# Weighted sums of two blocks in a row, behind the single-pass products of both blocks

## What is computed

```python
sim = jnp.einsum('bhid,bhjd->bhij', q * SCALE, k)          # n = 1024
sim = jnp.where(causal_mask, jnp.finfo(sim.dtype).min, sim)
attn = jax.nn.softmax(sim, axis=-1)
out = jnp.einsum('bhij,bhjk->bhik', attn, values)
```

## Time and profile before

| | us |
|---|---|
| median of 3 runs | 1012.2 |
| lowest, highest | 1009.75, 1013.5 |
| the profiled execution | 1008.53 |
| its span, first to last instruction | 1006.7 |

### The profile page before, as it was taken

How to read it: one execution, slowest core, us unless ns; L and a number is a source line. 1 busy time by engine, 2 the same in 40 slices (tenths; PEclk the granted TensorE clock), 3 DMA queues, 4 the chain that set the end, 5 groups by cost and what they waited for, 6 DMA issues and landing times.

```text
span 1006.7 us, 14712 instructions
## 1 busy us (share of the span) xinstructions
PE 946.7 (94%) x5620; PEld 734.5 (73%) x5620; DVE 684.6 (68%) x1051; ACT 392.1 (39%) x683; POOL 239.2 (24%) x261
## 2 busy tenths in 40 slices
PE   5879989999999999989999899999999999999997
PEld 3448868888755565689996687788876666659997
DVE  2555757546656778788876675665575767879786
ACT  5424556312266557510104346540204755761000
POOL 6211324123433214145610013220012201311000
PEclk9988999999999999999999999999999999999999
DMA  6112100252135430235541000012221000023663
GB/s 226 29 42 74 53 1 2 70 175 83 55 126 207 145 130 23 73 109 168 174 143 68 1 1 1 2 49 84 84 84 42 23 21 1 22 74 88 195 191 103
DMA packets 33848, 81.56 MB, mean 81 GB/s; under 512 B 5956, under 2 KB 10660, under 8 KB 33780
## 3 DMA queue, kind: packets, MB, share of 16 engines
q1 hardware_dynamic: 32500, 76.44, 23.4%
q10 hardware_dynamic: 1280, 4.20, 1.6%
HBM read 61.26 MB, written 19.20 MB: 80 GB/s over the span
## 4 chain that ended last, share of the span: by engine, by line
PE 73%; DVE 11%; ACT 4%; issue 4%; DMA 3%; POOL 2%; SPq 2%; ACTq 0%; DVEq 0%; POOLq 0%
PE ps L1054 17%; PE ps L1352 10%; PE ps L1289 6%; PE ps L1357 5%; PE ps L1204 4%; PE ps L1249 4%; DVE region L948 3%; PE ps L1062 3%; PE ps L1265 3%; PE ps L1156 3%; PE ps L1218 3%; PE ps L1171 2%; PE ps L1325 2%; PE ps L1326 2%; SPq L303 2%
## 5 line engine op out<-in xcount | busy, mean ns | idle before, releaser
L1289 PE MATMUL ps<-region 128*128 128x512 f32 (+3 forms) x384 | 161.4, 504 | 0.0
L927 DVE TENSOR_REDUCE region<-ps 128x1 f32<-128x512 f32 (+1 forms) x192 | 98.1, 550 | 65.7 <-PE ps L1268 65.7
L715 ACT ACTIVATE region<-ps 128x512 f32<-128x512 f32 x192 | 92.3, 487 | 125.1 <-PE ps L1328 113.6
L972 DVE COPY_PREDICATED region<-region,ps 128x512 f32<-128x512 uint32 x112 | 82.0, 736 | 71.9 <-PE ps L1054 71.3
L1352 PE MATMUL ps<-expert_hi,kst 128*128 128x256 f32 x512 | 126.1, 284 | 3.5 <-DVE kst L1002 2.5
L1352 PE MATMUL ps<-expert_lo,kst 128*128 128x256 f32 x512 | 124.4, 281 | 0.0
L1054 PE MATMUL ps<-expert_hi,wide_hi 128*128 128x512 f32 x256 | 102.6, 401 | 0.0
L1352 PEld LDWEIGHTS ps<-expert_hi,kst 128*128 128x128 f32 x512 | 97.2, 190 | 4.5 <-DVE kst L1002 2.9
L1054 PE MATMUL ps<-expert_hi,wide_lo 128*128 128x512 f32 x256 | 100.0, 391 | 0.0
L1054 PE MATMUL ps<-expert_lo,wide_hi 128*128 128x512 f32 x256 | 99.8, 390 | 0.0
L519 ACT ACTIVATE region<-ps 64x512 f32<-64x512 f32 (+4 forms) x146 | 80.9, 557 | 47.1 <-PE ps L1171 20.0
(11 more groups left out here) (143 smaller groups left out, 1797.0 us busy)
## 6 DMA issues: line engine op xcount, KB each, us to landing
region<-hot_rows SPq DMA_DIRECT2D x128, 128.0 KB, 3.4
expert_hi<-halves_kept SPq DMA_DIRECT2D x24, 512.0 KB, 3.7
expert_lo<-halves_kept SPq DMA_DIRECT2D x24, 512.0 KB, 4.8
halves_kept<-expert_hi SPq DMA_DIRECT2D x16, 512.0 KB, 2.7
halves_kept<-expert_lo SPq DMA_DIRECT2D x16, 512.0 KB, 3.9
expert<-in_value_experts SPq DMA_DIRECT2D x8, 512.0 KB, 5.0
expert<-in_output_experts SPq DMA_DIRECT2D x8, 512.0 KB, 5.1
gb<-gate_rows ACTq DMA_DIRECT2D x16, 256.0 KB, 3.8
```

The source lines that it names most:

```text
L715: act.activation(PT[:, g % RING, lo:CH], ps[:, 4 + g % 2, 0:CH - lo], ACT.Exp).then_inc(sem["pt_ready"], 1)
L927: dve.tensor_reduce(mx[:, i, at_mx:at_mx + 1], ps[:, max_bank(h, m), 0:w], AX.X, ALU.max).then_inc(sem["s_max"], 1)
L972: dve.copy_predicated(V3_heads[:, t], chosen.unsqueeze(3).broadcast_to([P, PAIRS3, 2, HD3]), ps[:, n % 4, :].rearrange("p (a i k) -> p a i ...
L1289: mm(ps[:, SUM_BANK[c], lo:CH], V3[:, j, h // 2, h % 2 * HD3:(h % 2 + 2) * HD3], PT[:, g % RING, lo:CH], start=(j == 0), stop=(j == TC * ( ...
```

## The change

In PE's loop over the blocks the call of weigh moves. Before, each block's transposed scores were followed at once by the sum of the block two before, and then by the projection, the scores and the row of maxima that the tables put there. Now a block with even n is followed by its projection and scores alone; a block with odd n by its projection and scores, then by the sums of the blocks three and two before it, then by the row of maxima. Every instruction of every engine stays, and the order on the other engines too.

```diff
                         last.then_inc(sem["st_ps"], 1)
-                        if g >= LAG:
-                            weigh(g - LAG)
                         if n in PROJECT_AT and h % 2 == 0 and h + 2 < H3:
                             project(h // 2 + 1, PROJECT_AT.index(n))
                         if h + 1 < H3:
                             for m in SCORES_AT.get(n, ()):
                                 scores(h + 1, m)
-                            if n == MAX_ROW_AT:
-                                max_rows(h + 1)
+
+                        if n % 2:
+                            for k in (g - 1 - LAG, g - LAG):
+                                if k >= 0:
+                                    weigh(k)
+                        if h + 1 < H3 and n == MAX_ROW_AT:
+                            max_rows(h + 1)
 
                 for g in range(H3 * NB - LAG, H3 * NB):
                     weigh(g)
```

## The result

| | before | after |
|---|---|---|
| median, us | 1011.3 | 1020.93 |
| lowest, highest, us | 1009.75, 1013.5 (4 runs) | 1018.82, 1023.04 (4 runs) |
| the profiled execution, us | 1008.53 | 1021.03 |
| its span, us | 1006.7 | 1019.2 |

Before's median is that of four runs, the three of the first table and one more. The change makes the kernel slower: the ratio of after to before is given as 1.0102, with a 95% interval of 1.0079 to 1.0125 (the two medians alone would make 1.0095). The spans of the two profiled executions differ by 12.5 us. The forecast was 1025, with 1014 to 1032 as its range, and slower as the likeliest sign.

The account below looks back on a forecast made before the run. The prediction took PE, busy 94% of the span, as the bound. Lost cover of 8.5 us in the second entry and 4.0 in the first made 12.5, added to a 1012.2 us median: about 1025, range 1014 to 1032.

Parts of the forecast that it names:

- What bounds the kernel: PE, busy 94% of the span; in the head stages reordering could remove at most 13 us of idle time.
- the price of a change of kind: Switching PE between single-pass and four-pass products: saving taken as 0, bounds 6 us saved to 2 us lost.
- (a): Projection 3, heads 0, 2, 4: a sum moves behind its wait for DVE's L940; 0.92 us lost each.
- (b): Transposed score 3, heads 0 to 6, waits for ACT's exponential 1; a sum moves behind it, about 0.9 us lost.
- (c): Next head's first score, heads 1, 3, 5, 6, waits for the second query copy; 0.7 us lost as a sum moves.
- (d): Score 3's existing wait for DVE's first maximum absorbs earlier losses: 0.8 us in heads 3 and 5, 1.1 in 6.
- Head 7: PE's wait for an exponential before transposed score 6 would go, covered by 0.9 us more of sums: -0.3 us.
- The first entry: First batch entry: 8.5 us less 0.8 and 0.3 for further waits, less 3.4 for L931, gives 4.0 us.
- L931's gain: First entry, heads 0 and 2: L931 on DVE ends before POOL's L399 starts, saving 1.7 us each.
- The other queues: DVE, ACT, POOL and SP keep their order; later signals for sums were costed at nothing.
- The second rival: Inputs reach ACT and DVE sooner, absorbing all losses except (a): about 1014 us; 10 in 100.
- The third: Rival: (d) absorbs no loss and L931 gains nothing, 24 us slower, about 1036 us; 10 in 100.

Follow-up runs that it names:

- e1: The changed kernel with the sums of blocks 8 and 9 each back behind its own block, the former before projection 3: 1016.57 us, ratio 1.0074 to before.
- e8: The kernel before with only projection 3 and the sum of block 8 exchanged, projection first: 1014.77 us, ratio 1.0043 to before.
- e2: The changed kernel with the sums issued at blocks 2 and 3 back behind their transposed scores, the rest in pairs: 1015.33 us, ratio 1.0058 to before.
- e4: The kernel before with only the last score of the next head moved ahead of the sum at n = 8: 1004.85 us, ratio 0.9958 to before.
- e3: The changed kernel with sums paired only at n = 0 and 1 and 4 to 9: 1008.88 us, ratio 0.9991 to before.
- e5: The kernel before with the last score (n = 8) and the row of maxima (n = 9) ahead of their sums: 1001.01 us, ratio 0.9897 to before.
- e7: The kernel before with sums halved by columns, first half between L1325 and L1326, second where the sum was: 1008.74 us, one execution.
- e9: e5 with score 3 moved from n = 4 to n = 5 and later scores packed closer: 1002.43 us, ratio 0.9932 to before.
- e6: The kernel before with sums halved by columns, both halves where the sum was, as control for e7: 1010.18 us, one execution.
- e10: e5 with DVE's multiplications L956 and L958 moved behind the first three maxima: 1001.42 us, ratio 0.9926 to before.

## Why the prediction came out as it did

**What bounds the kernel, and the price of a change of kind.** Right. PE has what it had to do, 13.2 of the 14.6 us lost are waits that the view of PE's waits names, and blocks without waits take the sum of their passes whether one, two or four changes of kind fall on them. The value of 0 was the sum's most important choice, since it left nothing against the waits. It came from one difference of starts in the last head, where nothing else could be in it.

**(a).** Right: 0.86 us at each projection 3 by the lag (0.92 forecast). e1 takes exactly this back, and e8 makes it alone.

**(b) and (c).** Right in place and size: 0.86 us in the heads that have (b) alone, 2.51 = 0.86 + 1.65 from head 0 to 1. Of the 1.65 some 0.13 is the wait at score 6, which the prediction did not have; (b) and (c) themselves are 1.5, against 1.6. e2 removes both waits.

**(d).** Right in size, wrong in mechanism. The heads 3 and 5 came to 1.59 and 1.40 against 1.6 because the step took 0.8 to 0.9 us off, and 0.78 in fact go at score 3 of head 3 (lag 10.39 at n = 4, 9.61 at n = 6). The 0.2 between 1.59 and 1.40 is what w6 behind the last score gains in head 5, as in e4. But the step said that losses of (a) to (c) alike are taken off. e8 shows that (a) is not; it came out right because (b) and (c) alone are larger than the wait. The prediction had not asked what DVE itself was held by: it listed the instructions in DVE's order and did not see that L956, with two operands in SBUF, ran for 1.75 us in before instead of 0.69. In head 6 only w2 is left over, as forecast, at 0.58 us instead of 0.4; the difference is the wait at score 6 that e2 shows. The prediction looked for DVE's first maximum alone, though every score from the fourth on waits for a maximum.

**Head 7.** Wrong, and with 0.85 to 0.87 us in each entry the largest miss: -0.3 forecast, +0.57 and +0.55 measured. The step was "0.9 us more of sums lie ahead of it after the change, and it goes". It is false by the diff alone: st6 is an even block, and ahead of an even block both kernels have issued the same sums (up to w3). PE's and ACT's timelines of after show the old wait where it was, with 0.17 us against the 0.16 of the earlier trace rows, and a second one that the step did not look for:

```profile
911.83 0.50 PE L1325 MATMUL ps<-qq,kst 128*128 128x512 f32 x1 [0.17 <-ACT region L715]
...
915.62 0.44 PE L1325 MATMUL ps<-qq,kst 128*128 128x384 f32 x1 [0.32 <-ACT region L715]
```

```profile
913.09 0.62 ACT L519 ACTIVATE wide_lo<-region 128x512 fp32r<-128x512 f32 x1
913.74 1.21 ACT L519 ACTIVATE region<-ps 64x512 f32<-64x512 f32 x2
914.97 1.09 ACT L715 ACTIVATE region<-ps 128x512 f32<-128x512 f32 x2
```

st9 takes the bank of st7, so it waits for exponential 7, which ACT does only behind the rounding and the evacuation. An odd block has one sum less ahead of it than before (w6 now comes behind st9), and its cover is 0.86 us thinner. The lag of head 7 is the same 0.54 to 0.57 us in e1, e2 and e3, which keep the pair at n = 9, and at most 0.02 in e4 and e5, which have none.

**The first entry.** L931's gain is right to the size: the mean of its 16 instructions falls from 459 to 163 ns (7.4 to 2.6 us in total), and the lag falls by 1.7 us in heads 0 and 2. That L940 would not be held instead, which the prediction took from one operand in PSUM, is right too. In after it ran for 1.21 us while POOL's L399 was on from 289.15 to 291.50:

```profile
288.55 0.16 DVE L931 TENSOR_TENSOR region<-region 128x4 f32<-128x4 f32 x1
...
290.19 1.21 DVE L940 SCALAR_TENSOR_TENSOR qx<-ps,const 8x1024 fp32r<-8x1024 f32 x1 [1.47 <-PE ps L1276]
...
289.15 2.35 POOL L399 TENSOR_TENSOR expert_lo<-expert,expert_hi 128x1024 fp32r<-128x1024 f32 x1 [9.29 <-ACT expert_hi L519]
```

The page SBUF — State Buffer of the Trainium skill (section SBUF: two separate sides) gives this as its rule, that the exclusive lock is taken by a DVE instruction with both inputs in SBUF, against a GpSimd one that reads SBUF. The traces agree for L931 (2.10 us, ending 0.02 us behind L399), L956 (ending 0.55 us behind L410) and L940 (1.21 us beside L399). The 5.4 us against 4.0 are head 7 again (0.9), head 2 (0.35) and head 4 (0.25). The last two come from st11 of the head before, which waits for exponential 9, and this stands on ACT behind a piece of the experts whose DMA lands late. With w8 no longer ahead of it, st11 waits 1.58 us in head 3, against 1.22 in before, and 1.46 us in head 1, where it did not wait in before. In head 2 the second projection's wait falls from 1.61 to 0.30 us, but this only pays for the new wait at st11, and (b), of which the prediction had left only 0.6 us there, stays whole.

**The other queues.** Costed at nothing; no row of ACT's waits contradicts it. ACT's exponentials wait for the scores alone (L1326 and L1328) in both traces, and for no sum.

**The total.** By the heads the forecast was 2.1 us too low (14.6 against 12.5). It was made up by 2.3 us of the output stage that nothing in the prediction foresaw, so that the span's 12.5 us equal the forecast 12.5 by luck within about 2 us. The median of 1020.9 lies 4 us under 1025, since I added the 12.5 to a median that lay 3.7 us above the profiled execution, while the changed kernel's profiled execution lies on its own median. The second rival (absorbed, 1014) fails at its own condition: st0 came no sooner, its lag in the second entry only grows, from 3.8 us in head 0 to 12.5 in head 7. The third (nothing absorbed and L931 gaining nothing, 1036) has both conditions against it.

## What to carry to other kernels

A product that is ready, standing in program order just ahead of one that waits for another engine, is cover; before regrouping work, list for each wait what stands ahead of it and for how long, and for even and odd steps apart. Put first what starts another engine's chain (the last score, the row of maxima) and behind it what nobody waits for (the sum): moving two such sums gave 1% (6.8 us by the heads), where grouping them by kind cost 1% (14.6 us by the heads). And before counting a wait as one that absorbs losses, follow its chain back to the first instruction it hangs on: it absorbs only what comes behind that one.

## What the runs showed of the hardware that was not expected

**One stream of products, two cadences.** In the output stage the same products of 256 columns (L1357 in before, L1360 in after) come in stretches at one of two rates. PE's timeline in before,

```profile
487.29 1.10 PE L1357 MATMUL ps<-expert_hi,qq 128*128 128x256 f32 x8
...
490.12 1.10 PE L1357 MATMUL ps<-expert_hi,qq 128*128 128x256 f32 x8
```

and in after:

```profile
492.50 1.07 PE L1360 MATMUL ps<-expert_hi,qq 128*128 128x256 f32 x8
...
495.22 1.07 PE L1360 MATMUL ps<-expert_hi,qq 128*128 128x256 f32 x8
```

A group of 24 products takes 2.83 us (118 ns each) in the one and 2.72 us (113 ns) in the other, both at a granted clock of 1.00. In before and after the rate changed behind a wait, behind the two transpositions (L1034) that stand between some groups, or at the end of a stretch at the lower clock. Of the 31 steps from group to group in the first entry's stage the last 24 take 69.1 us in before, 66.9 in after and e7, 67.0 in e1, e2, e5 and e9, and 69.4 in e3, e4, e6, e8 and e10. The 2.2 us between before and after are nearly all of the 2.3 by which their stages differ. The rate does not go with the order in the heads (e5 and e10 differ in DVE's order alone), and its cause is open; no run tried it, and with one profile a kernel it isn't shown whether a kernel keeps its rate. It is a reason to compare stages, not spans: at 2.2 us it is worth as much as a term of this sum.

**The same wait, with and without a lower clock behind it.** Early in that stage PE waits 2.25 us for ACT before L1034, in every one of the twelve kernels (at 449.10 in before). In nine of them the granted clock is 0.50, the level of 1.2 GHz, for about 3 us soon behind it, and the products of 256 columns come every 213 ns. The window of before:

```profile
449.80:452.50 2.70, 2.70 (x14) 0.50 0.94 364
```

In e4, e6 and e8 it stays at 1.00 behind the same wait. The first seven steps take 25.8 to 25.9 us in the nine and 24.3 in the three, 1.5 us less. Before and after both have it, so it has no part in their difference. Why the three have not is open.

**A long hold of DVE by POOL, off the place where it was looked for.** L956 takes 0.68 us free (e10). In heads 2 to 6 of the second entry of before, after, e2 and e5 it starts while L410 runs and ends 0.55 us behind it every time: 0.99 us long in heads 2 and 4 of before, 1.75 in heads 3 and 5, and 2.62 there in after.
